# Attention stage of a fused two-layer model: expert-weight splitting, query buffers, unrolled heads and the order of wo

## The reference

```python
x = x + attn(layernorm(x))     # 2 batches x 1024 tokens, 16 heads of 32: softmax(q k^T / sqrt(32) + causal) v, then @ Wo + bo
x = x + moe(layernorm(x))      # 32 experts of 192, top 8 of them: sum_e w_e * down_e(silu(gate_e x) * up_e x)
x = x + ssd(layernorm(x))
x = x + lut_ffn(layernorm(x))
```

## Time and profile before

| | us |
|---|---|
| median of 3 runs | 2573.71 (2566.74 to 2581.66) |
| the profiled execution | 2575.64 |
| its span, first to last instruction | 2574.1 |
| PE busy | 2334.5 (91%) |
| DVE busy | 1497.5 (58%) |
| ACT busy | 977.3 (38%) |
| POOL busy | 1094.5 (43%) |

### The profile page before, as it was taken

The page is one execution under the profiler, slowest core; times in us unless marked ns, Lnnn a source line. Parts: engine busy times, 40 slices in busy tenths (PEclk is TensorE's granted clock), DMA queues, the critical chain, the costliest instruction groups (busy, mean ns, idle before and its releaser), DMA issues. The chain is left out here.

```text
span 2574.1 us, 47582 instructions
## 1 busy us (share of the span) xinstructions
PE 2334.5 (91%) x12710; PEld 1773.7 (69%) x12712; DVE 1497.5 (58%) x3155; ACT 977.3 (38%) x2202; POOL 1094.5 (43%) x993
## 2 busy tenths in 40 slices
PE   7969998996756999999999779999989998999998
PEld 5855455443535989989989648888855664788886
DVE  6336556663566555555555457999256665655554
ACT  3114555453254444444444342222255553312221
POOL 3128888776002666666667501111166663000000
PEclk9978999998866999999999879999999999999999
DMA  5458999996355999999999834447499761000001
GB/s 178 122 175 311 346 338 329 341 326 252 116 204 145 245 283 281 258 265 273 271 263 221 149 129 148 168 163 232 141 217 225 166 151 38 13 25 25 25 9 66
DMA packets 263307, 491.18 MB, mean 191 GB/s; under 512 B 31889, under 2 KB 149137, under 8 KB 253458
## 3 DMA queue, kind: packets, MB, share of 16 engines
q1 hardware_dynamic: 197202, 272.17, 34.9%
q0 software_dynamic: 62976, 212.42, 29.4%
q10 hardware_dynamic: 3024, 5.29, 0.6%
HBM read 592.96 MB, written 198.79 MB: 308 GB/s over the span
## 5 line engine op out<-in xcount | busy, mean ns | idle before, releaser
L1431 PE MATMUL m_ps_u<-m_ring,m_xT_hi 128*128 x1280 | 370.4, 350 | 0.2 <-issue 0.2
L1399 POOL DMA_INDIRECT expert_sum<-x_res,token_of x160 | 257.1, 1607 | 182.9 <-DMA expert_sum<-x_res,token_of 66.3
L808 ACT ACTIVATE probs<-ps_c 128x512 f32<-128x512 f32 (+3 forms) x384 | 179.1, 491 | 208.7 <-PE ps_c L741 102.7
L1431 PEld LDWEIGHTS m_ps_u<-m_ring,m_xT_hi 128*128 128x128 f32 x1280 | 236.7, 190 | 1.2 <-issue 0.6
L1431 PE MATMUL m_ps_u<-m_ring,m_xT_lo 128*128 x640 | 216.9, 339 | 0.0
L1392 POOL DMA_INDIRECT m_xg<-x_rows,token_of x160 | 172.5, 1078 | 100.6 <-issue 92.3
L709 PE MATMUL ps_r<-k_st,q_st 96*128 96x512 f32 (+3 forms) x384 | 163.8, 433 | 53.4 <-DVE neg_max L838 22.4
L1878 PE MATMUL s_ps<-s_x_hi,s_w_hi 128*128 128x512 f32 x512 | 199.7, 390 | 1.6 <-POOL s_w_lo L1848 1.6
L1878 PE MATMUL s_ps<-s_x_lo,s_w_hi 128*128 128x512 f32 x512 | 199.3, 389 | 0.0
L1878 PE MATMUL s_ps<-s_x_hi,s_w_lo 128*128 128x512 f32 x512 | 199.2, 389 | 0.0
L2647 DVE TENSOR_TENSOR x_res<-f_ps_o,x_res 128x512 f32<-128x512 f32 x176 | 109.3, 684 | 143.4 <-PE f_ps_o L2540 143.4
(11 more groups left out here) (357 smaller groups left out, 5782.0 us busy)
## 6 DMA issues: line engine op xcount, KB each, us to landing
m_ring<-w_split SPq DMA_DIRECT2D x160, 1536.0 KB
m_ring<-w_split SPq DMA_DIRECT2D x160, 768.0 KB
w_split<-e_gu_parts POOLq DMA_DIRECT2D x32, 1536.0 KB
proj<-s_out SPq DMA_DIRECT2D x32, 1024.0 KB, 4.0
e_raw_gu<-w_experts POOLq DMA_DIRECT2D x32, 768.0 KB
w_split<-e_dn_parts POOLq DMA_DIRECT2D x32, 768.0 KB
e_raw_dn<-w_experts POOLq DMA_DIRECT2D x32, 512.0 KB
q_st<-q_parts SPq DMA_DIRECT2D x32, 256.0 KB
```

The lines of the kernel that those rows point to most:

```text
L808: nc.scalar.activation(probs[a][j % RING][:, :width], ps_c[(j * BATCH + a) % BUFS][:, :width], ACT.Exp, scale=SCALE).then_inc(exp_done, 1)
L1399: pool.indirect_dma_start(acc[j % 2], rows_at(j), y[j % TURNS], None, bounds_check=PADDED - 1, oob_is_err=True, compute_op=ALU.add).then_i ...
L1431: last = nc.tensor.matmul(ps_u[b % 2][:, :W_UP], x[b % 2][:, k, :], ring[:, first + k * GU_ROW:][:, bass.ds(place, W_UP)], start=(n == 0), ...
```

## The change

- POOL: the weights of two experts come as three blocks of 1536 columns: gate/up of the one, gate/up of the other, and the down weights of both, with the 64 rest rows of both in 128 partitions, no longer doubled. Each block has a buffer for the raw weights and one for both parts. A unit is now: cast 0, cast 1, subtract 0, subtract 1, store 0, load 0 of the next head, store 1, load 1, cast 2, subtract 2, four stores of down weights (pieces of 2 KB), load 2. The content and layout of `w_split` stay.
- wo is loaded in two halves and split after the first and the second head.
- q and k lie in DRAM so that a half of both batches is one run of 4 KB, and `q_st`, `k_st` the same.
- `q_st` has three buffers; q of head u+3 is loaded after the second half of y of head u is stored. k is issued after the 8th and the 12th chunk, as before.
- y is stored by halves, each with its own semaphore, and each copy waits for the same half's store of the head before.
- DVE: join, rounding and difference of the maxima are one-input reductions (`tensor_reduce`) over 1 or 2 elements in place of `tensor_tensor` and `tensor_copy`; one more in each `parts`, which writes the negated rounded value beside the maximum.
- PE, ACT, DVE and SP are written out for all heads; POOL keeps a loop for heads 2 to 13.

```diff
-            return qk["qk"[m // (MT // 2)]][h0:h0 + HT, part, :, g * GROUP:(g + 1) * GROUP]
+            return qk["qk"[m // (MT // 2)]][h0:h0 + HT, part, :, g % 2, g // 2, :]
...
+    Q_BUFS = 3
+    STORES = (1, 1, 4)
...
+        raw_all, parts_all = sb("e_raw", [P, UNITS_OF_PAIR, UNIT_W]), sb("e_parts", [P, UNITS_OF_PAIR, 2, UNIT_W], F32R)
+        raw, high, low = [[t(x) for x in range(UNITS_OF_PAIR)] for t in (lambda x: raw_all[:, x, :], lambda x: parts_all[:, x, 0, :], lambda x: parts_all[:, x, 1, :])]
...
+            def split_high(u, x, first):
+                pool.wait_ge(w_loaded[x], u * 16 + 16)
                 pool.sem_inc(turns_begun, 1)
-                if not start(it, e):
-                    pool.wait_ge(gu_stored[x], u * 16)
+                if not first:
+                    pool.wait_ge(w_stored[x], u * STORES[x] * 16)
                     pool.sem_inc(turns_begun, 1)
-                nc.gpsimd.tensor_copy(hi, raw_gu[x][:, :]).then_inc(gu_split, 1)
-                pool.wait_ge(gu_split, p * 2 + 1)
+                nc.gpsimd.tensor_copy(high[x], raw[x]).then_inc(high_done, 1)
+
+            def split_low(u, x):
+                pool.wait_ge(high_done, u * UNITS_OF_PAIR + x + 1)
                 pool.sem_inc(turns_begun, 1)
-                nc.gpsimd.tensor_tensor(gu_parts[x][:, GU:], raw_gu[x][:, :], hi.bitcast(F32), ALU.subtract).then_inc(gu_split, 1)
-                pool.wait_ge(gu_split, p * 2 + 2)
+                nc.gpsimd.tensor_tensor(low[x], raw[x], high[x].bitcast(F32), ALU.subtract).then_inc(low_done, 1)
+
+            def load_raw(u, x):
+                pool.dma_start(raw[x], w_raw[bass.ds(u, 1), x].rearrange("u p c -> p (u c)")).then_inc(w_loaded[x], 16)
...
+            def store_gate_up(u, x):
+                pool.wait_ge(low_done, u * UNITS_OF_PAIR + x + 1)
                 pool.sem_inc(turns_begun, 1)
...
+                pool.dma_start(w_split[bass.ds(2 * u + x, 1), :, :2 * W_GU].rearrange("e p c -> p (e c)"),
+                               parts_all[:, x, :, :].bitcast(F32).rearrange("p n c -> p (n c)")).then_inc(w_stored[x], 16)
+
+            def store_down(u):
+                pool.wait_ge(low_done, u * UNITS_OF_PAIR + 3)
                 pool.sem_inc(turns_begun, 1)
...
+                for x in range(2):
+                    dst = w_split[bass.ds(2 * u + x, 1), :, 2 * W_GU:2 * W_GU + 2 * D].rearrange("e p (n c) -> p (e n) c", n=2)
+                    pool.dma_start(dst, parts_all[:, 2, :, x * D:(x + 1) * D].bitcast(F32)).then_inc(w_stored[2], 16)
+                for n in range(2):
+                    dst = w_split[bass.ds(2 * u, 2), n * REST_E:(n + 1) * REST_E, 2 * W_GU + 2 * D:]
+                    pool.dma_start(dst, parts_all[:, 2, n, 2 * D:].bitcast(F32)).then_inc(w_stored[2], 16)
...
+            def split_pair(u, first, more):
+                split_high(u, 0, first)
+                split_high(u, 1, first)
+                split_low(u, 0)
+                split_low(u, 1)
+                for x in range(2):
+                    store_gate_up(u, x)
+                    if more:
+                        load_raw(u + 1, x)
+                split_high(u, 2, first)
+                split_low(u, 2)
+                store_down(u)
+                if more:
+                    load_raw(u + 1, 2)
+
+            for x in range(UNITS_OF_PAIR):
+                load_raw(0, x)
+            for u in range(E):
+                take_v(u, u, True)
+                split_pair(u, u == 0, True)
+                split_wo(u)
...
+            part = lambda n, u, i, j, half: qk[n][bass.ds(u, 1), i:j, :, half].rearrange("h a d b t -> (h a d) (b t)")
...
+            def load_q(u, half):
...
+            def store_y(u, half):
+                sp.wait_ge(y_done, u * 2 + half + 2)
+                cols = slice(half * HALF, (half + 1) * HALF)
                 for a in range(BATCH):
...
+                    toks = slice(a * T + half * HALF, a * T + (half + 1) * HALF)
+                    sp.dma_start(yT[u:u + 1, :, toks].rearrange("h d t -> (h d) t"), y_st[a * COL:a * COL + DH, cols]).then_inc(y_stored[half], 16)
+                    sp.dma_start(all_sums[u:u + 1, toks], y_st[a * COL + DH:a * COL + DH + 1, cols]).then_inc(y_stored[half], 16)
...
+                if u == 1:
+                    sp.wait_ge(wo_split, 2)
+                    load_wo(1)
+                if u + E < HEADS:
+                    sp.wait_ge(cols_done, u * PER_UNIT + 8 * BATCH)
+                    load_k(u + E, 0)
+                store_y(u, 0)
+                if u + E < HEADS:
+                    sp.wait_ge(cols_done, (u + 1) * PER_UNIT)
+                    load_k(u + E, 1)
+                store_y(u, 1)
+                if u + Q_BUFS < HEADS:
+                    for half in range(2):
+                        load_q(u + Q_BUFS, half)
...
-                    nc.vector.tensor_tensor(blocks, blocks, second[:, :, :], ALU.min).then_inc(joined, 1)
+                    nc.vector.tensor_reduce(pairs[:, :, :, 0], both_max[:, :, :, :], AX.X, ALU.min).then_inc(joined, 1)
                     dve.wait_ge(joined, u + 1)
                 if not (isinstance(it, int) and it == 0 and e == 0 and half == 0):
                     dve.wait_ge(turned, u * 2 + half)
-                nc.vector.tensor_copy(of_batch[:, :, :, 0], blocks).then_inc(parts_done, 1)
-                dve.wait_ge(parts_done, u * 4 + half * 2 + 1)
-                nc.vector.tensor_tensor(of_batch[:, :, :, 1], blocks, of_batch[:, :, :, 0].bitcast(F32), ALU.subtract).then_inc(parts_done, 1)
+                nc.vector.tensor_reduce(pairs[:, :, :, 1].bitcast(F32R), pairs[:, :, :, 0:1], AX.X, ALU.max, negate=True).then_inc(parts_done, 1)
+                nc.vector.tensor_reduce(of_batch[:, :, :, 0], pairs[:, :, :, 0:1], AX.X, ALU.max).then_inc(parts_done, 1)
+                dve.wait_ge(parts_done, u * 6 + half * 3 + 2)
+                with nc.allow_low_precision(reason="one difference, rounded once to the type that the products read"):
...
-                if half == 0:
-                    dve.wait_ge(y_stored, (u + 1) * 64)
+                dve.wait_ge(y_stored[half], (u + 1) * 64)
```

More of the change, by code:

```diff
@@ L563, in _, with take_v @@
             pool.wait_ge(consts, CONSTS)
[L564 to L574, removed]
+            def take_v(u, h, first):
+                if not first:
@@ L595, in split_gate_up @@
[L595 to L602, removed]
-                pool.sem_inc(turns_begun, 1)
-                if not (start(it, e) and x == 0):
-                    pool.wait_ge(dn_stored, p * 16)
-                    pool.sem_inc(turns_begun, 1)
-                nc.gpsimd.tensor_copy(rest, raw_dn[x][:, D:]).then_inc(dn_split, 1)
-                nc.gpsimd.tensor_copy(hi, raw_dn[x][:, :D]).then_inc(dn_split, 1)
-                pool.wait_ge(dn_split, p * 4 + 2)
+                nc.gpsimd.tensor_tensor(low[x], raw[x], high[x].bitcast(F32), ALU.subtract).then_inc(low_done, 1)
@@ L650, in load_q, with load_k @@
                 for row, i, j in ((0, 0, 2), (2, 0, 1)):
[L651 to L653 removed]
+                    sp.dma_start(q_st[u % Q_BUFS][row * DH:(row + j - i) * DH, half, :, :].rearrange("p b t -> p (b t)").bitcast(F32), part("q", u, i, j, half)).then_inc(loaded, 16)
+            def load_k(u, half):
+                loaded = (k_low_loaded, k_up_loaded)[half][u % E]
@@ L682, in _ @@
-            sp.sem_inc(y_stored, 64)
-            for e in range(E):
-                load_q(0, e, 0, low_loaded[e])
-                load_k(0, e, 0, low_loaded[e])
-                load_q(0, e, 1, q_up_loaded[e])
-                load_k(0, e, 1, k_up_loaded[e])
-            with sp.Fori(0, BODIES - 1) as it:
-                body(it, False)
-            sp.dma_start(raw_wo[:, :, :], wo.rearrange("(k p) d -> p k d", p=P)).then_inc(wo_loaded, 16)
-            body(BODIES - 1, True)
-            sp.wait_ge(y_stored, 64 * (HEADS + 1))
+                    sp.dma_start(k_st[u % E][row * DH:(row + j - i) * DH, half, :, :].rearrange("p b t -> p (b t)").bitcast(F32), part("k", u, i, j, half)).then_inc(loaded, 16)
@@ new lines, in _ @@
+            for half in range(2):
+                sp.sem_inc(y_stored[half], 64)
+            for half in range(2):
+                load_q(0, half)
+                load_k(0, half)
+            for half in range(2):
+                load_q(1, half)
+                load_k(1, half)
+            for half in range(2):
+                load_q(2, half)
+            load_wo(0)
+            for u in range(HEADS):
+                if u == 1:
[10 more added lines that the diff above has]
+                if u + Q_BUFS < HEADS:
+                    for half in range(2):
+                        load_q(u + Q_BUFS, half)
@@ L694, in _ @@
+            for half in range(2):
+                sp.wait_ge(y_stored[half], 64 * (HEADS + 1))
         @block.tensor
@@ L781, in _ @@
                     turn_lower(0, 0)
-            body(0, True, False)
-            with pe.Fori(1, BODIES - 1) as it:
```

(17 more changed lines are left out.)

147 lines of the change are left out of this document (54 added, 93 removed).

## The result

| | before | after |
|---|---|---|
| median, same chip (9 runs each) | 2573.71 us | 2593.69 us (2587.57 to 2600.73) |
| profiled execution, its span | 2575.64, 2574.1 | 2594.85, 2593.2 |
| mean granted clock | 0.945 | 0.939 |

The account below looks back on a forecast made before the run. DMA was taken to bound attend after the change, at 25.6 us a head. Start 189, 15 turns 384, last 23.5, landing 6: end at 602 instead of 628.5 us; about 2549 us profiled, median 2547, range 2522 to 2578.

Parts of the forecast that it names:

- Two such are 14 to 16 us from the first issue: POOL's burst in attend: two store-and-load pairs, 4.7 MB, land within 14 to 16 us; turn 22.4 to 24.4, under 25.6 us.
- C: Rival, chance 0.11: in attend, loads behind the burst land later than 19.2 us; at 21 us turns take 29.4, total 2601 us.
- C's other half: In attend, k's load stands behind the same burst and stalls PE; sign: over 20 us of row-product waits; rival's chance 0.11.
- The down stores turn from 6 KB rows to 2 KB pieces: DMA in attend: smaller pieces of down weights cost between 0 and +1.5 us a head, 1.57 MB at 277 GB/s.
- wo first: POOL in attend: wo's splitting moves to heads 0 and 1, with 4 us to spare; landing, about 6 us, replaces it: nothing gained.
- All work after it: After attend, 1946 of the span's 2574.1 us is other code, which the diff doesn't touch.
- Unrolled heads: PE, DVE and ACT in attend: 7 turns are lost, counted as 0, though more code must be fetched.
- POOL's own unit: POOL in attend: take, casts, subtractions, issues and gaps sum to 21.5 us a head, saving 5.7 us.
- PE's head without waits: PE in attend: 27.3 us a head fall to about 24.0 us, the clean head.
- the y store's and q's waits gone: DVE and PE in attend: 19.9 us of y-store waits and 9.6 us of q waits go.
- small reductions: DVE in attend: 7 unstalled reductions of 0.2 us take 1.4 us a head against 2.7; worth 0 to 10 us in all.
- The DMA pace: All queues in attend: 24.9 us of transfers a head, 25.6 us at 97% share, as the bound after the change.

Follow-up runs that it names:

- e1: The changed kernel with each head's two [2, 64, 512] rest-row stores made four stores of one expert's 64 rows: 2576.48 us, ratio to before 0.9993.
- e7: e2 with wo split last, after unit 15, its second half loaded into the freed first weight buffer: 2556.95 us, ratio to before 0.9936.
- e6: e2 plus 102 increments of an unused semaphore in SP's program, moving SP's later code: 2548.66 us, ratio to before 0.9911.
- e2: e1 with POOL casting, subtracting, storing and loading each weight block by itself, one after another: 2562.56 us, ratio to before 0.9941.
- e3: The changed kernel with POOL's old splitting of expert weights, wo still after heads 0 and 1: 2596.96 us, ratio to before 1.0061.
- e5: The kernel before with 154 increments of an unused semaphore in SP's attention program, moving later code: 2584.61 us, ratio to before 1.0050.
- e8: The changed kernel with POOL's block-by-block order alone, keeping the [2, 64, 512] rest-row stores: 2560.47 us, ratio to before 0.9950.
- e4: The kernel before with POOL's new weight splitting alone, wo last as before: 2621.14 us, ratio to before 1.0153.
- e9: e11 with each unit's blocks in the order down, gate/up 0, gate/up 1: 2550.35 us, ratio to before 0.9894.
- e11: e7 with padding of SP's program by increments of an unused semaphore: 2555.24 us, ratio to before 0.9899.

## Why the prediction was wrong

**Where the time was to come from.** Predicted and measured start of the next stage, in the terms of the sum:

| us | predicted | measured |
|---|---|---|
| first load landed, splitting starts | 189 | 192.6 |
| 15 units | 384 (25.6 each) | 411.4 (27.4) |
| last unit | 23.5 | 24.9 |
| from POOL's last issue on | 6 + 4.8 (4.8 as before) | 17.1 |
| sum | 607.3 | 646.0 |

The units are counted here from the first cast of one to the first cast of the next, since the sum starts with the first load.

1. *"Two such are 14 to 16 us from the first issue ... so bytes and not latency set the pace, just."* This step failed, and with it the forecast: the 14 to 16 us were too short. Where block 1's cast waited, in 13 units, its load landed 16.3 to 22.2 us after the first store of the unit before was issued, 19.1 us in the mean, where C decides at 19.2. In the unit shown it is 20.2 us (341.35 to 361.5), and the next first store follows 28.4 us after the first, where C had 29.4 for 21 us. Block 2 then waits as well, which C had not. But the burst alone doesn't break the pace: with 64-row stores (e1) the same distance is 17.6 us in the mean and the unit 25.7 us, as forecast. It took the stores of point 2 with it. Why one such burst takes longer than twice the one of the earlier trace rows is open: that estimate left out the loads of q and k that fall into the longer burst, but the distance is 16.3 us in the last unit, when those have ceased (591.63 to 607.90), and also 16.7 and 16.9 us in two units that have them. I gave C 0.11 because the margin of 3 us looked like evidence; the earlier trace rows had already shown lateness of 10 us, and that row should have decided. C's other half, PE stalled by k, came small in the change (5.9 us, under the sign of 20) and larger in e1 (15.8 us).
2. *"The down stores turn from 6 KB rows to 2 KB pieces: between 0 and +1.5 us."* The cost of the new stores was looked for in their piece size; it lay in the number of engines. The rest stores ran at 68 GB/s for 8 us, and cost 27.4 us of waits at block 2; on top of the burst they are the 1.5 us a unit between e1 and the change. The rule on the engines of a transfer was at hand, and the shape [2, 64, 512] stands in the diff.
3. *"wo first ... nothing gained."* It cost. The first two units took 26.6 and 31.7 us instead of 25.6 each (35.2 and 31.8 from one take of v to the next, with the first load in it), since POOL had nothing "to spare behind DMA" there: besides its own 22.1 us each pays a wo half (3.4 us) and waits for loads, the second also 3.4 us for its half of wo. And the end, "about 6 us", is 9.9 us of landing (628.9 to 638.8) and a drain until 642.2. Before, the wo subtraction of the earlier trace rows covered the landing (the last packet of POOL's queue ends at 624.6 us), and the drain ended 1.9 us after it. e7 puts the loss of the position by itself at only 1.1 us, once landing is quick.
4. *"All work after it ... is other code."* This assumption cost 12.2 us in the profile, some 7 to 8 of them shown to be SP's loop. So did *"Unrolled heads: I count 0; more code must be fetched"*: I looked for the fetch inside the stage, where there is none to see; it appears in a loop of SP 300 us later.
5. Right: POOL's own unit (21.5 predicted; 603.40 - 579.57 less a wait of 1.77 is 22.1 measured); PE's head without waits (24.0, and 22.9 to be had); the y store's and q's waits gone; small reductions near 0.2 us (18.4 us / 16 = 1.15 us a head against 1.4). The Trainium skill's rule that `tensor_reduce` does not contend for the shared port pair (SBUF — State Buffer, "Practical consequences") agrees: the mean over the stage is 157 to 172 ns.
6. The DMA pace itself was nearly right, once the order lets DMA have it. e6 from 276 to 574 us:

```profile
276.00:574.00 298.00, 286.31 (x1669) 159.32 (x1665) 176.35 (x403) 162.68 (x348) 260.20 (x217) 0.98 0.99 357
```

At share 0.99 a unit takes 24.7 us, and 27.2 once (25.6 predicted, 24.9 us at 97%); 24.7 us is also POOL's own unit there, with eleven DMAs and six gaps instead of two, so the two bounds can't be told apart in it. With both cures the next stage starts at 607.0 us (e2), where the forecast had it, in part by errors that cancel: its first units are late as in 3.

Of the miss of 45.9 us in the profiled execution (2594.85 against 2549), 38.7 lie in `attend`: 27.4 in the pace of the 15 units (20.2 in the 13 from the third on, points 1 and 2; 7.2 in the first two, point 3), 6.3 at the end, 3.6 in the first load and 1.4 in the last unit. 6.4 lie behind it: +12.2 in the experts, -5.8 elsewhere, which no run explains (the rest is rounding of the sum).

## What to carry to other kernels

When DMAs are batched, walk every buffer's load from its place in the queue to its first use, with all the other queues' traffic of that stretch, and take the margin as a cost if it is only a few us: bytes saved are worth nothing if the engine that issues the next ones is waiting. Where a view names no releaser for a wait, compare its end with the landings of the loads that the instruction needs. Read the outermost counts of each new DMA as you read its bytes. A change in one stage's instruction count can slow a loop in another: compare the instruction queue's packets and the gaps at loop branches of both profiles before you look for a cause in the data.

## What the runs showed of the hardware

- A loop of 322 recorded instructions on SP pays 3.4 to 6.6 us at each turn or 0.0 to 0.7 us, by where it stands in the program: moved by about 154 instructions it paid (change, e1, e2, e3, e5, e7, e8), by 0 or 256 it did not (before, e4, e6, e9 to e11). The period in between was not tried. The packets of the instruction queue were 57 and 59 (change, e5) against 19 and 18 (before, e6).
- A store of two experts' 64 rows, 256 KB, ran at 34 GB/s (half of the 68), with mostly two data packets under way (half of the four). With rest stores of 64 rows on each side, e1's end looks so instead:

```profile
603.80:608.00 4.20, 0.00 (x0) 0.00 (x0) 0.00 (x0) 0.00 (x0) 0.00 (x0) 0.50 0.84 252
```

- GpSimd's drain at a stage's end took 1.9 to 6.1 us with nothing left to land, more where more DMAs had been issued per unit (8, 9 or 11 DMAs); the cause is open.
